# One program block for layer 1's attention and experts, in eight-slot head groups

## The reference, cut to what matters

```python
def _L1_attn_ref(x, ln_scale, ln_bias, wq, wk, wv):          # 16 heads of 16
    xn = _layernorm(x, ln_scale, ln_bias)
    ...
    scores = jnp.einsum('bhid,bhjd->bhij', q, k)
    probs = jax.nn.softmax(scores / jnp.sqrt(jnp.float32(HIDDEN_DIM)), axis=-1)
    out = jnp.einsum('bhij,bhjd->bhid', probs, v)
    out = out.transpose(0, 2, 1, 3).reshape(bs, sl, -1) + xn
    return out

def _L1_ffn_ref(x, Wr, rb, W1, W2, W3, Ws1, Ws2, Ws3):       # 8 experts, 2 per token
    ...
    h = jnp.einsum('bsd,edh->bseh', x, W1) * jax.nn.silu(jnp.einsum('bsd,edh->bseh', x, W3))
    expert_out = jnp.einsum('bseh,ehd->bsed', h, W2)
    out = jnp.einsum('bsed,bse->bsd', expert_out, w_full)
    ...
```

## Time and profile before

| | us |
|---|---|
| median of 3 runs | 2083.85 (2071.47 to 2100.62) |
| the profiled execution | 2093.61, its span 2091.9 |
| layer 0 norm and choice | 3.7 to 116 of the span |
| layer 0 mixer and experts | 116 to 730 |
| layer 1 prepare and route | 730 to 1030 |
| layer 1 attention | 1030 to 1575 |
| layer 1 experts | 1575 to 2041 |
| finish | 2041 to 2092 |

### The profile page before, as it was taken

The page is one execution under the profiler, slowest core; times in us unless marked ns, Lnnn a source line. Parts: engine busy times, 40 slices in busy tenths (PEclk is TensorE's granted clock), DMA queues, the critical chain, the costliest instruction groups (busy, mean ns, idle before and its releaser), DMA issues. The chain is left out here.

```text
span 2091.9 us, 24658 instructions
## 1 busy us (share of the span) xinstructions
PE 1698.2 (81%) x8146; PEld 1098.6 (53%) x8146; DVE 1174.3 (56%) x2114; ACT 850.8 (41%) x1509; POOL 528.8 (25%) x579
## 2 busy tenths in 40 slices
PE   4459999999996699999168878888876999999960
PEld 2337677676774465555122223222225888888850
DVE  3436655666554434333566677777743665566635
ACT  1124555445552122221025566565653445445421
POOL 1122443435432312211134410000001333333330
PEclk8679999999998799999557899998977999999985
DMA  3434644565332634442165533232304556555537
GB/s 126 147 111 101 152 103 105 136 151 141 81 86 51 212 134 161 150 161 101 45 143 136 143 98 90 76 86 72 85 16 132 139 125 150 141 148 132 133 61 241
DMA packets 223458, 251.08 MB, mean 120 GB/s; under 512 B 35984, under 2 KB 172688, under 8 KB 223376
## 3 DMA queue, kind: packets, MB, share of 16 engines
q1 hardware_dynamic: 193616, 208.54, 33.6%
q0 software_dynamic: 29760, 41.50, 11.2%
HBM read 153.34 MB, written 96.10 MB: 119 GB/s over the span
## 5 line engine op out<-in xcount | busy, mean ns | idle before, releaser
L1244 DVE TENSOR_REDUCE a_neg_max<-a_bank 128x1 f32<-128x512 f32 x512 | 328.6, 684 | 100.9 <-PE a_bank L1147 82.6
L1224 ACT ACTIVATE a_prob<-a_bank 128x512 f32<-128x512 f32 x512 | 278.7, 598 | 257.4 <-PE a_bank L1158 236.3
L1158 PE MATMUL a_bank<-a_qa,a_ka 50*128 50x512 f32 x512 | 137.7, 534 | 87.1 <-ACT a_prob L1224 57.0
L1476 POOL DMA_INDIRECT fs<-e_y,e_token x92 | 143.2, 1557 | 243.6 <-issue 232.3
L1147 PE MATMUL a_bank<-a_ka,a_qa 48*128 48x512 f32 x512 | 130.3, 503 | 42.9 <-DMA a_va<-v 30.7
L1167 PE MATMUL a_bank<-a_prob,a_va 128*32 128x512 f32 x1024 | 162.5, 765 | 1.2 <-ACT a_prob L1224 1.2
L1577 DVE TENSOR_TENSOR e_h<-e_bank,e_sg 128x512 f32<-128x512 f32 x92 | 63.6, 692 | 167.1 <-ACT e_sg L1542 167.1
L1158 PEld LDWEIGHTS a_bank<-a_qa,a_ka 50*128 50x128 f32 x512 | 51.4, 196 | 199.6 <-ACT a_prob L1224 107.2
L1542 ACT ACTIVATE e_sg<-e_bank 128x512 f32<-128x512 f32 x92 | 55.0, 597 | 222.1 <-PE e_bank L92 222.1
L648 POOL DMA_INDIRECT f<-e_ye,c_slot_row x64 | 100.9, 1577 | 75.2 <-issue 50.1
L1465 POOL COPY e_token<-e_xg 128x4 uint32<-128x4 uint32 x23 | 5.5, 237 | 422.5 <-DMA e_xg<-xs 371.6
(11 more groups left out here) (311 smaller groups left out, 4100.2 us busy)
## 6 DMA issues: line engine op xcount, KB each, us to landing
e_raw<-in_W SPq DMA_DIRECT2D x69, 512.0 KB
e_raw<-in_w SPq DMA_DIRECT2D x48, 512.0 KB, 5.3
a_qa<-qk SPq DMA_DIRECT2D x192, 64.0 KB
a_ka<-qk SPq DMA_DIRECT2D x192, 64.0 KB
xs<-c_pad SPq DMA_DIRECT2D x23, 516.0 KB
e_xg<-xs SPq DMA_DIRECT2D x23, 516.0 KB, 3.7
qk<-p_hi SPq DMA_DIRECT2D x32, 256.0 KB, 2.0
qk<-p_lo SPq DMA_DIRECT2D x32, 256.0 KB, 2.0
```

What stands on the lines that cost most here:

```text
L1158: nc.tensor.matmul(SB[(c + s) % 3][:], ka[q][rows, p, j * P:(j + 1) * P], qa[q][rows, p, :], start=True, stop=True).then_inc(s_ps, 1)
L1224: nc.scalar.activation(prob[j][:, 2 * p + s, :], SB[(c + s) % 3][:], ACT.Exp, scale=float(D) ** -0.5).then_inc(p_done, 1)
L1244: nc.vector.tensor_reduce(neg_max[:, g % 2, at_:at_ + 1], MB[(c + s) % 3][:], AX.X, ALU.max, negate=True).then_inc(mx_done, 1)
L1476: nc.gpsimd.indirect_dma_start(f_rows, bass.IndirectOffsetOnAxis(token[u][:, t:t + 1], 0), y[:, t, :], None, compute_op=ALU.add).then_inc( ...
```

## The change

`layer1_attention` and `layer1_experts` are replaced by `layer1_attend_and_experts`. It has one loop over the 32 head groups g, and each group has eight slots, one for each `scores(g, u)`. Groups 0 to 7 hold attention alone. In groups 8 to 30 the slots also hold the pieces of expert group e = g - 8: its up matmuls (gate and value apart), and the down matmuls of e - 1. Group 31 has attention and the last down matmuls.

- PSUM: one pair of banks M for the maxima, also for the transposes of the rows and of the maxima, one pair S2 for the scores, and one bank each for the output OB, the down product YB, GATE and VALUE. VectorE reduces and ScalarE exponentiates a whole pair (1024 elements) in one instruction. Scores of slot u + 1 wait for the exp of slot u, and maxima m + 1 for the reduction of m.
- prob has two tiles in place of four; q, k and v three buffers in place of four.
- silu(gate) is made of tanh: VectorE forms (tanh(gate / 2) + 1) * gate, and the factor 0.5 is folded into the routing weights.
- Low parts: of w3 and w1 on GpSimd (before on VectorE), of w2 on VectorE. The weighting of the rows moves from VectorE to ScalarE. GpSimd's scatter-adds come in two halves.
- GpSimd adds the attention output to `k.xa_all` itself (`add_o`, between the batches of the row scatter and then once per group); at1 is gone.
- x1 goes to HBM in `layer1_prepare` and comes back in `finish`, whose loads stand ahead of the store and whose first add is gone.
- `layer0_norm` has eight buffers of x in place of two, so that loads do not wait for the normalisation.

```diff
-    x, xn = [sb(f"x{u}", [P, T, D]) for u in range(2)], [sb(f"xn{u}", [P, T, D]) for u in range(2)]
+    x, xn = [sb(f"x{u}", [P, T, D]) for u in range(NB)], [sb(f"xn{u}", [P, T, D]) for u in range(2)]
...
-                sp.dma_start(x[n % 2][:], at(x_b, n)).then_inc(x_in[n % 2], 16)
+                sp.wait_ge(x_in[n % 2], 16 * (n // 2))
+                sp.dma_start(x[n][:], at(x_b, n)).then_inc(x_in[n % 2], 16)
...
-                sp.wait_ge(xn_done, n + 1)
                 if n + 2 < NB:
                     load_x(n + 2)
+                sp.wait_ge(xn_done, n + 1)
                 sp.dma_start(at(xn_b, n), xn[n % 2][:]).then_inc(xn_out[n % 2], 16)
...
+                    sp.wait_ge(x1_done, n + 1)
+                    sp.dma_start(at(x1_b, n), x1[:]).then_inc(x1_out, 16)
...
-                own.step(v.tensor_tensor(k.weight[:, i, :], ex[:, i, :], top[:], ALU.mult))
+                own.step(v.scalar_tensor_tensor(k.weight[:, i, :], ex[:, i, :], 0.5, top[:], ALU.mult, ALU.mult))
...
+    G, NU, NR = NB * NQ, 2 * T, 3
...
+    FIRST = G - 1 - NG
...
+    M, S2 = [R.ctx.enter_context(nc.psum_tensor(R.tag + n, [P, 2, 512], F32)) for n in ("max_bank", "score_bank")]
+    OB, YB, GATE, VALUE = R.banks(4)
...
+            load_qk(0)
+            load_qk(1)
+            load_v(0)
+            max_rows(0)
+            load_v(1)
+            for g in range(G):
+                e = g - FIRST
+                if g + 2 < G:
+                    load_qk(g + 2)
+                if group(e + 1):
+                    load_w(0, e + 1)
+                    load_w(1, e + 1)
+                if g + 2 < G:
+                    load_v(g + 2)
+                if g + 1 < G:
+                    max_rows(g + 1)
+                if group(e + 1):
+                    load_w(2, e + 1)
+                    if e + 1 == 0:
+                        load_x(0)
+                if group(e + 2) and e + 1 >= 0:
+                    load_x(e + 2)
...
+            def low_w(i, e):
+                pool.wait_ge(w_hi, 3 * e + i + 1)
+                dst = (w3, w1)[i][e % 2]
+                nc.gpsimd.tensor_tensor(dst[1][:], raw[i][:], dst[0][:].bitcast(F32), ALU.subtract).then_inc(w31_lo, 1)
...
+            for b in range(NB):
+                scatter_rows(b)
+                if b:
+                    add_o(b - 1)
+            added = NB - 1
+            for g in range(G + 2):
+                e = g - FIRST
+                if group(e - 2):
+                    combine(e - 2, 1)
+                if e >= -1:
+                    while added < min(g, G):
+                        add_o(added)
+                        added += 1
+                if group(e - 1):
+                    combine(e - 1, 0)
+                if group(e + 1):
+                    low_w(0, e + 1)
+                    low_w(1, e + 1)
+                    marks(e + 1)
...
+            for g in range(G):
+                e = g - FIRST
+                scores(g, 0)
+                maxima(g + 1, 4)
+                if group(e):
+                    up_gate(e, 0)
+                    up_value(e, 0)
+                maxima(g + 1, 5)
+                scores(g, 1)
+                if g:
+                    weigh(g - 1, 3)
+                if group(e - 1):
+                    down(e - 1, 0)
+                maxima(g + 1, 6)
+                scores(g, 2)
+                if group(e):
+                    up_gate(e, 1)
+                maxima(g + 1, 7)
+                if g:
+                    transpose_o(g - 1)
+                if group(e):
+                    up_value(e, 1)
+                scores(g, 3)
+                if group(e - 1):
+                    down(e - 1, 1)
+                transpose_max(g + 1)
+                scores(g, 4)
+                weigh(g, 0)
+                if group(e):
+                    up_gate(e, 2)
+                maxima(g + 2, 0)
+                if group(e):
+                    up_value(e, 2)
+                maxima(g + 2, 1)
+                scores(g, 5)
+                weigh(g, 1)
+                if group(e - 1):
+                    down(e - 1, 2)
+                maxima(g + 2, 2)
+                scores(g, 6)
+                if group(e):
+                    up_gate(e, 3)
+                maxima(g + 2, 3)
+                if group(e):
+                    up_value(e, 3)
+                scores(g, 7)
+                weigh(g, 2)
+                if group(e + 1):
+                    transpose_x(e + 1)
+                if group(e - 1):
+                    down(e - 1, 3)
...
+            def exps(g, u):
+                j, p = divmod(u, 2)
+                act.wait_ge(s_ps, 2 * (NU * g + u + 1))
+                if T * g + j >= 2 and p == 0:
+                    act.wait_ge(pv_ps, T * g + j - 1)
+                nc.scalar.activation(prob[j % 2][:, 2 * p:2 * p + 2, :], S2[:], ACT.Exp, scale=float(D) ** -0.5).then_inc(p_done, 1)
...
+            def tanh(e, f):
+                act.wait_ge(gate_ps, FC * e + f + 1)
+                act.wait_ge(h_done, FC * e + f)
+                nc.scalar.activation(tg[:], GATE[:], ACT.Tanh, scale=0.5).then_inc(tg_done, 1)
...
+            def hidden(e, f):
+                dve.wait_ge(tg_done, FC * e + f + 1)
+                nc.vector.scalar_tensor_tensor(tg[:], tg[:], 1.0, GATE[:], ALU.add, ALU.mult).then_inc(act_done, 1)
+                dve.wait_ge(up_ps, FC * e + f + 1)
+                dve.wait_ge(act_done, FC * e + f + 1)
+                dve.wait_ge(h_lo, FC * e + f)
+                nc.vector.tensor_tensor(h[:], VALUE[:], tg[:], ALU.mult).then_inc(h_done, 1)
...
+                maxima(g + 1, 4)
+                if group(e):
+                    hidden(e, 0)
+                maxima(g + 1, 5)
+                if group(e):
+                    low_h(e, 0)
+                maxima(g + 1, 6)
+                maxima(g + 1, 7)
+                if g:
+                    divide(g - 1)
+                if group(e):
+                    hidden(e, 1)
+                split_max(g + 1)
+                if group(e):
+                    low_h(e, 1)
+                maxima(g + 2, 0)
+                if group(e):
+                    hidden(e, 2)
+                    low_w2(e)
+                maxima(g + 2, 1)
+                if group(e):
+                    low_h(e, 2)
+                maxima(g + 2, 2)
+                maxima(g + 2, 3)
+                if group(e):
+                    hidden(e, 3)
+                if group(e + 1):
+                    low_x(e + 1)
+                if group(e):
+                    low_h(e, 3)
...
+            for b in range(NB):
                 sp.wait_ge(y_done, b + 1)
-                sp.dma_start(at(out_b, b), y[u][:]).then_inc(y_out[u], 16)
-                if more:
-                    sp.dma_start(fs[u][:], at(fs_b, b + 2)).then_inc(in_[u], 16)
-                    sp.dma_start(ao[u][:], at(at_b, b + 2)).then_inc(in_[u], 16)
-
-            with sp.Fori(0, NB // 2 - 1) as j:
-                for u in range(2):
-                    turn(2 * j + u, u, True)
-            for u in range(2):
-                turn(NB - 2 + u, u, False)
+                if b + 2 < NB:
+                    load(b + 2)
+                sp.dma_start(at(out_b, b), y[b % 2][:]).then_inc(y_out[b % 2], 16)
```

711 lines of the change are left out of this document (323 added, 388 removed).

## The result

The changed kernel takes 2103.2 us (median of 20 runs, 2092.4 to 2115.6) against 2084.7 for the kernel before on the same chip: a ratio of 1.0088, 95% interval 1.0070 to 1.0107. It is 0.9% slower. The prediction said 1988 us, range 1938 to 2055. The profiled execution of the changed kernel has a span of 2113.9 us; the prediction's span was 1995.5, so 118.4 us have to be found. This execution is the slowest of the 20, 12.5 us over their median.

A forecast was written before the change was run, and what follows sets the result against it. TensorE was taken to bound the merged stage: expert work from 1231, 23 combined groups of 30 us to 1921, last group, tail and finish to 2001.5, less 6 for layer 0: span 1995.5 us; forecast 1988 us, range 1938 to 2055.

The forecast's parts named there:

- The combined group: Groups 8 to 30, attention plus one expert group each: 30 us per group, 23 of them 690 us.
- TensorE's own work: Combined group: sum of TensorE's matmuls and transposes at full clock, 27.9 us.
- Wait (1): Combined group: maxima(g+2, 2) waits for a reduction that VectorE does behind hidden(e, 2) and low_w2; about 0.4 us.
- wait (3): Combined group: maxima(g+2, 4) waits for low_x of the next rows; 0.8 us.
- wait (2): Combined group: transpose_o waits for the copy behind exp 2; 0.3 us.
- No row of this trace shows that.: Combined group: said of the exclusive lock between two-SBUF-input VectorE operations and SBUF-reading GpSimd ones; left out of the 30 us.
- The rival with the lock: Combined group: GpSimd's low_w and VectorE's two-input operations take turns; 31.5 to 34 us, typically 2045 us; chance 0.18.
- a stretched one means the lock: Sign in the combined groups: low_h should stay at 0.68 us beside low_w; a longer low_h would show the lock.
- The slower rival: Merged stage: small waits keep TensorE's clock low; at 0.8 a group is 37 us, kernel 2149 us; chance 0.06.
- The start: Up to group 8's expert work: begins at 1231, less 6 for layer 0.
- 17.2 us against 13.8 before, some 20.5 at half clock. I take 18.5: Groups 0 to 7, attention alone: time per group set by the maximum chain on single banks, taken as 18.5 us.
- The scatter was to decide the start: Before group 8: the last scattered row lands at 1223, expert work starts at 1231, attention having waited some 20 us.

The follow-up runs named there:

- mended order: The changed kernel with GpSimd's first low_w of a combined group waiting until VectorE has done low_h of slice 2; 2039.5 us, ratio 0.9775 to the kernel before.

## Why the prediction was wrong

**What bounds the kernel.** The reading that the merged stage would be bound by TensorE holds: 94% busy in the changed kernel, 98.6% with the mended order. The merge itself does what was argued. Its two sizes were not right, and a rival was given too little.

**The combined group, 30 us predicted, 34.15 measured.** Four terms; the first two errors cancel in part (2.6 us more, 1.6 less), so that the 30 us without the lock, 30.97 measured, were nearer than their terms:

| term | predicted | measured | from |
|---|---|---|---|
| TensorE's own work | 27.9 | 30.5 | mended order, 30.51 busy |
| small waits | 2.1 | 0.46 | 0.21 and 0.25 in a group |
| delay by the lock | 0 | 1.7 | 32.65 against 30.97 |
| slow clock behind it | 0 | 1.5 | 34.15 against 32.65 |

*TensorE's sum was mis-sized.* I took up matmuls at 0.227 us, from twelve in a row. In the merged order only six stand together in three of the four slices, and the first of each six takes 0.33 to the next (1755.92 to 1756.26 above, behind a maximum pair) where the others take 0.23: 12.5 us and not 10.9 per group. The same holds for pairs (0.33 next to each other, 0.43 before other work; 6.2 for 5.8) and for down matmuls (6.4 for 5.8). Rates read from long runs of one kind were applied to short ones.

*None of the three small waits came as priced.* Wait (1) was put at 0.4 and is 0.21 on its own; wait (3) at 0.8 is 0.25; wait (2), for copy_o, is not there.

*"No row of this trace shows that."* This is the step that failed: the lock and the clock behind it stood in the forecast at nothing. The rival with the lock was named, with its mechanism, its rows in the order and the right number of collisions: "at my slot times only one low_h meets a low_w". That sentence stood as an argument against it, and one collision was enough. It had 0.18. The sign that the prediction gave for it ("a stretched one means the lock") is what the trace shows. The Trainium skill (SBUF — State Buffer, the section on who interferes with whom) states it plainly: a VectorE instruction with two SBUF inputs contends with a GpSimd instruction that reads SBUF, and the other one blocks for the whole instruction. The trace agrees: 0.69 became 2.89 beside 2.39. The row of before that I set against it (GpSimd's 0.724 beside a VectorE multiply with an input in PSUM) could not speak against it, as the last form measured here shows: with a PSUM input there is no lock. A row that differs in the very point of the rule is no evidence.

*Its price was half of what it is.* I priced the lateness alone, 1.5 us for one collision, which measured 1.7. TensorE's wait of 1.6 us let the clock fall, and 1.5 us more went in slow matmuls. The slower rival had the clock as its mechanism, but as something even over the whole stage (0.87 or 0.8); it came as a stretch behind one wait.

**The start, 1225 predicted, 1250.5 measured.** First scores came at 1059.8, for 1061 less the 6 of layer 0: 4.8 us late. Then the step "17.2 us against 13.8 before, some 20.5 at half clock. I take 18.5" failed: 23.5 to 24.1 us at clock 0.55, eight groups in 190.7 us for 148. Of these 43 us the forecast had 22 in hand, as a wait for the scatter that did not come. Worked through slot by slot with the durations of the changed kernel's rows (a reduction 1.15 after its matmuls land, a pair 0.33 or 0.59, a weighing 0.99 or 1.87), I get 17.4 us at full and 24.4 at half clock, an estimate. The half-clock value is also measured, 24.41 us at 0.50, so the predicted one was 4 us too low, because I had stretched only the maximum chain and left out that four weighings of 1.9 us stand in TensorE's queue inside it. And I had assumed a clock between the two from a stage of before that had three banks, where now single banks make TensorE wait in each slot. The groups of 20.4 and 24.4 us with the same work show the clock as a cause. The full-clock value of 17.2 stays unmeasured: no group with single banks and without filler ran at more than 0.75.

*The scatter was to decide the start, with 20 us of waiting.* It did not: attention was the later, and the scatter waited for it through the output adds. That the gained start is "worth nothing where the scatter decides" was wrong for the same reason: with attention the later, an earlier start of attention is not lost.

**Last group and tail** took 34.6 for 30.5: in group 31 TensorE waits 1.15, 1.20 and 1.15 us for an exp at the single pair of score banks, and 1.63 and 0.72 for a copy of the output. The finish took 48.8 for 50. **Layer 0** gave 9 us for 6, with an interval that holds 6.

**The range.** It held the lock rival's 2045 and ended at 2055. The two misses are independent: 25 us at the start alone would have left 2013, well inside; 90 us in the groups alone 2078, beyond it by 23. (Its inner 1957 to 2025 is 1955 to 2028 if its terms are added in full; nothing hangs on that.) The upper end was the typical case of one rival, and held neither its clock term nor anything beside it.

## What to carry to other kernels

Before moving an elementwise step to GpSimd, list VectorE's operations with two SBUF inputs (and its fast copies from SBUF) that can fall beside it, and make the later of the two wait by a semaphore, or give VectorE an operand in PSUM: here one wait in a queue was worth 64 us. A short wait on TensorE is to be priced at about twice its length where it lets the clock fall, and a stage whose matmuls wait in each slot should be priced at half clock too, with all that stands in TensorE's queue stretched (here 24.4 us per group, for 20.4 at 0.75). Times per matmul read from long runs of one shape are too short for an order that alternates.

The kernel with the later low_w and two pairs of maximum banks is 3.8% faster than the kernel before, 2001.6 us; with the two row buffers and four filler transposes per slot, which are not shown to add to that, it measured 4.6%, 1992.7 us. The merge was worth making, and one collision per group and one pair of banks hid it.

## What the runs showed of the hardware

- VectorE's fp32 copy and tensor_scalar of 512 elements from SBUF to SBUF take 0.37 us alone (tensor_tensor 0.63) and are held by a GpSimd tensor_tensor too; so are two SBUF inputs with the output in PSUM. Operations with an input in PSUM are not, nor are two SBUF inputs by a GpSimd memset. Where both keep issuing, both lose: GpSimd's three went from 6.94 to 8.30 us.
- GpSimd's fp32 tensor_tensor of 1024 elements takes 2.39 us, VectorE's 1.22.
- The same wait of 1.61 us was followed by a slow stretch in most groups and by none in a few (34.15 and 32.65 us for the same work). What decides it, these runs don't show.
- In attention alone the granted clock changes from group to group in one execution, and the group's time with it: 20.44 us at 0.75 and 24.41 at 0.50 with single banks, 15.37 at 1.00 and 19.35 at 0.65 with two pairs.
- The block's first matmul lies anywhere between 1025.7 and 1035.8 in kernels whose code up to there is the same. Profiled spans differ by that much before the part under study begins, so stages were compared from that matmul on.
